# Products of the expert, input and output weights issued as two halves, with every place in the order chosen anew

## The reference, cut to what matters

```python
xz = einsum('bld,ed->ble', layernorm(x), in_proj_w)      # 512 -> 1024
x_ssm, z = split(xz, 2, axis=-1)
x_conv = silu(causal_conv4(x_ssm) + conv_b)
B, C, dt = split(einsum('bld,ed->ble', x_conv, x_proj_w))  # 16, 16, 1
delta = softplus(dt); A = -exp(A_log)                    # A: 512 x 16
h = exp(delta * A) * h + delta * B * x_conv              # a scan over 1024 tokens
y = (einsum(h, C) + D * x_conv) * silu(z)
x = x + einsum('bld,ed->ble', y, out_proj_w)
t = layernorm(x)
w, idx = top2(softmax(t @ router_w.T + router_b))        # 8 experts, weights to sum 1
x = x + sum_k w_k * (t @ expert_weights[idx_k])          # each expert 512 x 512
```

## Time and profile before

| | |
|---|---|
| median of 3 runs | 2839.52 us (2834.74 to 2843.43) |
| the profiled execution | 2832.45 us |
| its span, first to last instruction | 2830.4 us |
| TensorE busy, matmuls | 2346.3 us, 83% |
| VectorE busy | 2261.3 us, 80% |
| GpSimd busy | 1810.6 us, 64% |
| ScalarE busy | 1483.6 us, 52% |
| mean granted TensorE clock | 0.913 of 2.4 GHz |

### The profile page before, as it was taken

The page is one execution under the profiler, slowest core; times in us unless marked ns, Lnnn a source line. Parts: engine busy times, 40 slices in busy tenths (PEclk is TensorE's granted clock), DMA queues, the critical chain, the costliest instruction groups (busy, mean ns, idle before and its releaser), DMA issues.

```text
span 2830.4 us, 34513 instructions
## 1 busy us (share of the span) xinstructions
PE 2346.3 (83%) x9510; PEld 1362.2 (48%) x9510; DVE 2261.3 (80%) x3144; ACT 1483.6 (52%) x2417; POOL 1810.6 (64%) x1418
## 2 busy tenths in 40 slices
PE   5667767698998889798897989798887989798886
PEld 2435344454545555454545545454544545454442
DVE  3888888899888989898888989888888988868400
ACT  3554554456474656556564656546564656534231
POOL 2555665657575776757685776757686676748542
PEclk8778777699998999899998999899998999889998
DMA  3772421223233443435343443435344343436875
GB/s 121 250 261 87 138 78 35 80 85 127 83 109 108 121 141 112 124 108 161 98 138 115 115 142 103 136 102 167 96 128 126 107 150 108 127 112 181 215 228 153
DMA packets 192570, 366.27 MB, mean 129 GB/s; under 512 B 22912, under 2 KB 22912, under 8 KB 192384
## 3 DMA queue, kind: packets, MB, share of 16 engines
q1 hardware_dynamic: 144272, 263.26, 29.0%
q0 software_dynamic: 28672, 67.13, 10.9%
q10 hardware_dynamic: 19440, 33.69, 3.3%
HBM read 212.73 MB, written 151.26 MB: 129 GB/s over the span
## 4 chain that ended last, share of the span: by engine, by line
PE 44%; DVE 21%; issue 15%; POOL 8%; ACT 8%; DMA 2%; DVEq 1%; SPq 0%; POOLq 0%; ACTq 0%
PE work L1179 32%; DVE acc L1021 8%; DVE h L1013 8%; PE hT L1184 8%; POOL u L728 6%; ACT decay L874 3%; DVE xc L1044 3%; PE work L1184 2%; PE work L1239 1%; POOL x_out L828 1%; DVE xc L1070 1%; ACT xn L891 1%; ACT x L952 1%; POOL row_scratch L813 1%; ACT L874 1%
## 5 line engine op out<-in xcount | busy, mean ns | idle before, releaser
L728 POOL TENSOR_TENSOR u<-xc,b_ring 128x1024 f32<-128x1024 f32 x512 | 1228.4, 2408 | 747.0 <-DVE h L1013 609.6
L874 ACT ACTIVATE decay<-dt,neg_a 128x512 f32<-128x512 f32 x1024 | 699.6, 688 | 689.6 <-DVE h L1013 661.4
L1184 PE MATMUL hT<-ident,h 128*128 128x128 f32 x4096 | 663.2, 297 | 386.5 <-DVE acc L1021 280.6
L1184 PEld LDWEIGHTS hT<-ident,h 128*128 128x128 f32 x4096 | 503.2, 151 | 658.7 <-DVE acc L1021 328.6
L1021 DVE SCALAR_TENSOR_TENSOR acc<-hT,ct,acc 128x512 f32<-128x512 f32 x960 | 699.6, 729 | 65.4 <-PE hT L1184 63.2
L1013 DVE TENSOR_TENSOR_SCAN h<-decay,h_last,u 128x512 f32<-128x512 f32 x512 | 652.0, 1275 | 113.5 <-ACT decay L874 76.9
L1179 PE MATMUL work<-w_exp,xeT 128*128 x1528 | 709.1, 608 | 35.0 <-issue 25.8
L1013 DVE TENSOR_TENSOR_SCAN h<-decay,u 128x512 f32<-128x512 f32 x512 | 620.6, 1214 | 98.7 <-ACT decay L874 57.2
L1179 PE MATMUL work<-xnT,w_in 128*128 128x512 f32 x1024 | 492.8, 627 | 0.7 <-issue 0.7
L1179 PEld LDWEIGHTS work<-w_exp,xeT 128*128 128x128 f32 x1528 | 279.7, 193 | 342.7 <-issue 342.6
L1179 PEld LDWEIGHTS work<-xnT,w_in 128*128 128x128 f32 x1024 | 198.5, 204 | 207.1 <-issue 207.1
(11 more groups left out here) (143 smaller groups left out, 1840.7 us busy)
## 6 DMA issues: line engine op xcount, KB each, us to landing
b_ring<-b_scratch SPq DMA_DIRECT2D x256, 256.0 KB
xe<-row_scratch SPq DMA_DIRECT2D x165, 256.0 KB
result_scratch<-ye SPq DMA_DIRECT2D x165, 256.0 KB
row_scratch<-x_out ACTq DMA_DIRECT2D x32, 1024.0 KB, 4.9
x<-in_x SPq DMA_DIRECT2D x66, 256.0 KB, 5.0
x_scratch<-x SPq DMA_DIRECT2D x64, 256.0 KB, 3.2
xn<-in_x SPq DMA_DIRECT2D x62, 256.0 KB, 3.0
x_out<-x_scratch SPq DMA_DIRECT2D x44, 256.0 KB, 3.9
```

The source lines that it names most:

```text
L728: nc.gpsimd.tensor_tensor(out=u[:, at:at + 2, :], in0=xc[:, half, 2 * k:2 * k + 2, :], in1=b_ring[:, n % ROWS:n % ROWS + 1, :].to_broadcas ...
L874: nc.scalar.activation(decay_bank[g % 2][:], dt[:, half, :], ACT.Exp, scale=neg_a[:, c, n:n + 1]).then_inc(decay_ready, 1)
L1184: last = nc.tensor.transpose(ps[:, k * P:(k + 1) * P], tile(k), ident[:])
```

## The change

The products of `project`, `z_project`, `out_project` and `expert` are issued in two steps. The first has contraction steps 0 and 1 and keeps its name; it takes the bank and makes the waits. The second, with `_end` behind its name, has steps 2 and 3 and raises the semaphore. Each `_end` step has places of its own in the tables, so other work of TensorE can stand between the halves. `xp_project`, `router` and the others stay whole.

All the other places change as well. Of the tables two rows show the form:

```diff
-        "expert": [12.67, 15.2, 18.98, 27.8, 33.46, 35.02, 40.91, 47.06, 52.97, 58.29, 61.96, 64.89],
+        "expert": [12.67, 15.33, 18.98, 27.8, 33.16, 35.02, 40.91, 47.06, 52.1, 58.89, 61.63, 65.09],
+        "expert_end": [13.41, 15.35, 19, 28.22, 33.16, 35.04, 40.93, 47.08, 54.79, 58.91, 62.38, 66.67],
...
+            def begin(ps, left, right):
+                for k in range(C // 2):
+                    nc.tensor.matmul(ps, left(k), right(k), start=(k == 0), stop=False)
+
+            def end(ps, left, right):
+                for k in range(C // 2, C):
+                    last = nc.tensor.matmul(ps, left(k), right(k), start=False, stop=(k == C - 1))
+                return last
+
+            def bank_of(j, key):
+                bank_no, _ = use_of(j, key)
+                return work_bank[bank_no], work_full[bank_no]
...
-                        product(ps[:], lambda k: sz[:, 1 - half, k, q * P:(q + 1) * P], lambda k: w_out[:, k, :]).then_inc(full, 1)
+                        begin(ps[:], lambda k: sz[:, 1 - half, k, q * P:(q + 1) * P], lambda k: w_out[:, k, :])
+                    elif s[0] == "out_project_end":
+                        q = s[1]
+                        ps, full = bank_of(j, ("out_project", q))
+                        end(ps[:], lambda k: sz[:, 1 - half, k, q * P:(q + 1) * P], lambda k: w_out[:, k, :]).then_inc(full, 1)
...
-                        expert = pe.value_load(tile_expert[g % 2][at:at + 1, 0:1], min_val=0, max_val=E - 1)
+                        expert_no[tile] = pe.value_load(tile_expert[g % 2][at:at + 1, 0:1], min_val=0, max_val=E - 1)
```

More of the change, by code:

```diff
@@ new lines, in mamba_moe_kernel @@
+        "residual": [12.66, 14.75, 17.76, 18.91],
+        "rstd2": [16.9, 22.4],
+        "store_x1": [8.89, 13.21, 17.59, 19.33],
+        "norm2": [17.91, 18.33, 23.19, 23.34],
+        "norm2_T": [17.86, 18.75, 24.1, 25.01],
+        "norm2_evict": [18.84, 21.22, 25.49, 26.68],
+        "router": [18.97, 19.86, 25.51, 26.98],
+        "gate_logits": [19.7, 22.39, 26.93, 28.37],
+        "gate_top": [30.33],
+        "gate_exp": [32.64],
+        "gate_sum": [34.96],
+        "gate_weights": [37.73],
@@ L237, in closing_steps @@
             steps += [("rows_T", i + 1)] * (i + 1 < last) + [("rows_load", i + 3)] * (i + 3 < last)
-            steps += [("rows_evict", i + 1)] * (i + 1 < last) + [("expert", i), ("expert_evict", i), ("rows_store", i)]
+            steps += [("rows_evict", i + 1)] * (i + 1 < last) + [("expert", i), ("expert_end", i), ("expert_evict", i), ("rows_store", i)]
             steps += late("late_store", 3) if i == (first + last) // 2 else []
@@ L1210, in steps_of @@
                             pe.wait_ge(project_loaded, 16 * PROJECT_LOADS)
-                        product(ps[:], lambda k: w_in[:, k, m * P:(m + 1) * P], lambda k: xnT[:, k, :]).then_inc(full, 1)
+                        begin(ps[:], lambda k: w_in[:, k, m * P:(m + 1) * P], lambda k: xnT[:, k, :])
+                    elif s[0] == "project_end":
+                        m = s[1]
+                        ps, full = bank_of(j, ("project", m))
+                        end(ps[:], lambda k: w_in[:, k, m * P:(m + 1) * P], lambda k: xnT[:, k, :]).then_inc(full, 1)
                     elif s[0] == "z_project":
@@ L1216, in steps_of @@
                             pe.wait_ge(weights_loaded, 16 * WEIGHT_LOADS)
-                        product(ps[:], lambda k: w_in[:, k, m * P:(m + 1) * P], lambda k: xnT[:, k, :]).then_inc(full, 1)
+                        begin(ps[:], lambda k: w_in[:, k, m * P:(m + 1) * P], lambda k: xnT[:, k, :])
+                    elif s[0] == "z_project_end":
+                        m = C + s[1]
+                        ps, full = bank_of(j, ("z_project", s[1], s[2]))
+                        end(ps[:], lambda k: w_in[:, k, m * P:(m + 1) * P], lambda k: xnT[:, k, :]).then_inc(full, 1)
                     elif s[0] == "xp_project":
```

192 lines of the change are left out of this document (96 added, 96 removed).

## The result

| | before | after |
|---|---|---|
| median | 2838.86 us (4 runs, 2834.74 to 2843.43) | 2799.24 us (4 runs, 2797.68 to 2800.39) |
| the profiled execution, its span | 2832.45, 2830.4 us | 2800.39, 2798.2 us |

A forecast was written before the change was run, and what follows sets the result against it. VectorE, with the least slack, was taken to bound the blocks, TensorE the packed window. Terms summed to 48 us; two thirds, 32, off the profiled 2832.45 gave 2800, plus 7 to the median: 2808 us, range 2770 to 2850.

The forecast's parts named there:

- Behind the window: After the first router product, the rest of a block: waits shrink, 3.85 us gained in even blocks, 3.2 in odd.
- S4.2: VectorE's sum for state 4, quarter 2: its 1.01 us wait for transposes of h goes, 1.0 us gained.
- Other waits for transposes: VectorE's sums behind the window: five further idle pieces, 1.8 us together, shrink by 0.7 us.
- dt, -0.55 and silu of x, -0.3: Two scans waiting for ScalarE's decays, behind dt's table load and behind the silu of x: 0.55 and 0.3 us less.
- u: Two scans idling 0.94 and 1.22 us for GpSimd's u: 0.5 us less as scatters and gathers are dealt out anew.
- Handover: First scan of the next block idles 2.31 us; the stall moves to the block's last scan, 0.8 us less.
- The gather: GpSimd's gather, now ahead of the four gates, delays the first out product 1.7 us in even blocks, 0 in odd.
- The packed window: First out product to first router product, TensorE never idle: VectorE's waits inside count nothing; window 0.2 us shorter.
- The clock rival: Even blocks' start: the split expert product lets TensorE's clock fall, 24 us off the forecast, 2832 us; chance 0.06.
- TensorE's busy time: Whole program: each extra change from transposes back to a product costs 0.1 us, so busy time grows 17 us.
- Blocks 1 and 2: Early blocks, counted as one ordinary even and odd pair: 6 us gained together.
- The end: Last block gains a tenth of its idle time, 5 us; the tail behind it 0, between -4 and +4.

The follow-up runs named there:

- e3: The changed kernel with the first gather of a block put back behind the four gate products; 2793.70 us, ratio 0.984.
- e12: e11 with decay 4.2 ahead of the second expert product's eviction and the first second norm, two groups of transposes moved too; 2791.27 us, ratio 0.9831.
- e8: The old kernel's places with products in halves, but the expert products whole; 2842.24 us, ratio 1.0014.
- e11: The changed kernel with gather behind gates, old end, and even blocks' first expert product moved ahead of the packed stretch; 2776.35 us, ratio 0.9783.
- e4: The changed kernel with one tile load put behind the load of B of state 2 in the last scan block; 2802.25 us, ratio 0.9874.

## Why the prediction came out, term by term

- **Behind the window, -3.85 in an even block: -2.0 came, and -2.4 of -3.2 in an odd one.** The pieces follow, by block 10.
- **S4.2, -1.0: wrong in what is late next.** The stall went. I wrote that VectorE had "a sum, a scan and a tap" before it needs T4.3; the next scan, 6.0, overwrites the h that T4.3 reads, and the tap had been moved behind it. 1.19 us stand there: nothing gained, in even and odd blocks alike.
- **Other waits for transposes, -0.7.** They fell from 1.8 to 0.4, 1.4 us less, in all 2.4 with S4.2. Scans that wait for transposes have 1.4 in place of 0.3 (handover aside), so 1.3 of the 1.7 forecast for both came.
- **dt, -0.55 and silu of x, -0.3.** 1.07 to 0.45, and 2.50 to 2.30: right.
- **u, -0.5.** Nothing came: behind the window has 0.94 and 1.22 us, and 0.53 not among them; after, 1.64 and 1.23, 0.2 more. Another 0.63 stands inside the window.
- **Handover, -0.8.** 2.31 us went from the first scan, 1.27 stand before scan 15.3: -1.0, as foretold in both places. New there is 0.52 before scan 14.0, which waits for a decay.
- **The gather, +1.7 in even blocks: right as a mechanism** (e3: 1.5 at out0), and mis-sized as a whole: out0 slipped by 2.9. Of the other 1.3 us, 0.5 are gates that end later and 0.8 are transposes in a row ahead of out0, T1.3 the last, 0.85 to 0.97 us apart where they are 0.44 apart at the full clock (e3, block 10). I had taken T1.3 out of the window and added nothing for it ahead of out0, and had no term for the clock. In odd blocks out0 slipped 0.5 on the mean, 0.7 in block 11, where I had 0.2 earlier: one of my own signs of being wrong.
- **The packed window, nothing for what lies inside:** 27.4 us against 27.5 expected. In e12 2.5 us of VectorE's idle time went from one place in it and came back at others, and the window kept its length.
- **The clock rival** had the right subject and the wrong place and sign. Even blocks fell from 0.99 to 0.97, from 9 to 30 us and not at the expert; odd blocks rose, and in block 11 out0 went from 5.3 to 3.7 us and its window gave 2.1 us. That an expert product at the start of an even block is enough to hold the clock there does not stand: in e8 it is whole, and block 10 starts it at the lower clock. No run here settles the rule of the Trainium skill that I weighed (page "TensorE: Matmul & The Clock Gate", "Part 4: PE-mode transpose"): in e8 one and the same order holds the clock once and loses it once.
- **TensorE's busy time, +17 us: it fell by 13.** The cost of 0.1 for each change from transposes to a product was a misreading. Behind transposes a half takes 1.72 us from start to start, as behind another half; it takes 1.82 only where TensorE idled just before it (a whole product 3.44 and 3.53). At the full clock the split costs TensorE nothing. Its busy time fell most in block 1, from 115.35 to 110.74 us.
- **Blocks 1 and 2, taken as ordinary pairs, -6: they gave 16.7.** I had windows of blocks 10, 11 and 15 only. At a clock of 0.78 a product is longer, and so was the wait behind one: 2.74 us before S4.2 in block 1 for 1.01 in block 10. Halves and places brought 3 to 4 us each there, without the other.
- **The end, -5 and 0: +10.2.** "A tenth of the idle time" was no reading of rows. One part of it could have been seen in the order: the load ahead of B in SyncE's queue.

The whole sum was 48 us and 32 came. Against my terms the even blocks lack 12.6 us, the end 15.2 and the odd blocks 1.1; blocks 0 to 2 gave 13.1 more, 2.4 of it in block 0, where 3 us come and go between kernels that have the same order in it (last section). The third that I left out, 16 us, happens to be the difference: that is luck. I had left it out because a stall that goes uncovers the wait behind it; that holds for S4.2 and for the sums, but not for the end, which had another cause, nor for blocks 1 and 2, which gave more than their terms. The reading that VectorE has the least slack is also too strong for the even block: in the earlier trace rows TensorE is busy 137.83 us of it and VectorE 137.72.

## What to carry to other kernels

A split and the places chosen for it are one thing: each without the other lost 44 or 83 us against both together, so that testing a part told little of the whole. Price the parts of a program that differ from the steady state (first blocks, last block, tail) from their own windows, and look there first for a load that waits in a queue ahead of one that is needed soon. Where an engine is packed, moving what waits for it renamed the waits (e12); moving its work ahead of the stretch helped (e11), up to the point where something else bounds the stretch.

## What I had not expected of the hardware

- The same instructions take 156.5 or 159.6 us in two blocks of one execution (e8), as TensorE's granted clock over the first 9 us is 1.00 or 0.81; the idle time ahead differed by 0.35 us, and the kernel before keeps 1.00 with the longer of the two. The kernel before has it too: its block 12 takes 157.9 us with 0.84 from 9 to 30 us, the other even blocks 156.1 to 156.5 with 0.92.
- Block 0 takes 145 us in seven of the fourteen profiles and 148 to 149 in the others (147.9 the least), among them pairs with the same order up to there (145.0 in e3, 148.0 in e4). What decides it stayed open; in a comparison of 0.1% it must be looked at.
